# A state-space scan on eight cores: the C-product of one state moves from VectorE to GpSimd, the carry copy from GpSimd to ScalarE

## The reference

```python
def step(h, inp):                      # L = 2048 steps, d = 2048 channels, N = 16 states
    dt_t, B_t, C_t, x_t = inp
    A_bar = jnp.exp(jnp.minimum(dt_t[..., None] * A, 20.0))
    B_bar = dt_t[..., None] * B_t[:, None, :]
    h = A_bar * h + B_bar * x_t[..., None]
    y_t = jnp.einsum('bdn,bn->bd', h, C_t)
    return (h, y_t)
...
y = y + x_ssm * D[None, None, :]
y = y * jax.nn.silu(z)
out = jnp.einsum('ble,de->bld', y, W_out) * jax.nn.sigmoid(output_gate)
```

## Time and profile before

| | |
|---|---|
| time, 2 runs | 8252.49 and 8291.18 us, median 8271.84 us |
| the profiled execution's own time | 8309.93 us |
| its span, slowest core (5) | 8308.3 us; the other cores 8185.8 to 8300.3 us |
| DVE, POOL, PE, ACT busy | 45%, 37%, 26%, 14% of the span |
| granted TensorE clock, mean | 0.594 to 0.600 by core |
| scan stages, first to last block | 1828 to 7192 us |

### The profile page before, as it was taken

How to read it: one execution, slowest core, us unless ns; L and a number is a source line. 1 busy time by engine, 2 the same in 40 slices (tenths; PEclk the granted TensorE clock), 3 DMA queues, 4 the chain that set the end, 5 groups by cost and what they waited for, 6 DMA issues and landing times.

```text
span 8308.3 us, 37246 instructions; the slowest of 8 cores (8185.8 to 8308.3 us)
## 1 busy us (share of the span) xinstructions
PE 2185.6 (26%) x5698; PEld 533.1 (6%) x5698; DVE 3780.1 (45%) x3767; ACT 1148.8 (14%) x1666; POOL 3074.0 (37%) x3119
## 2 busy tenths in 40 slices
PE   0005657500000100346031007420400445034732
PEld 0001112100000000001010001000100000010101
DVE  0431111128888667586208676632468576201010
ACT  0001112102121111121101112110111121100000
POOL 0111111136666555463316454433355454300011
PEclk9998877655555555555565555555755555565556
DMA  8557665540000421020451200215321020433233
GB/s 112 161 148 155 147 143 130 125 81 8 9 9 10 58 51 32 14 51 7 72 81 40 62 23 13 48 28 83 81 53 32 14 50 12 72 84 78 41 62 70
DMA packets 851754, 529.48 MB, mean 64 GB/s; under 512 B 677762, under 2 KB 782210, under 8 KB 850882
## 3 DMA queue, kind: packets, MB, share of 16 engines
q0 software_dynamic: 122384, 262.35, 16.1%
q1 hardware_dynamic: 710706, 247.99, 13.8%
q10 hardware_dynamic: 18432, 16.79, 0.7%
HBM read 241.59 MB, written 144.97 MB: 47 GB/s over the span
## 4 chain that ended last, share of the span: by engine, by line
DVE 31%; DMA 31%; PE 11%; issue 9%; DVEq 7%; SPq 5%; POOL 3%; POOLq 3%; ACT 1%; ACTq 1%
DVE Hbz L215 20%; DVE ubz L215 7%; DVEq L213 7%; PE mid_ps L215 5%; PE big_ps L215 5%; DMA q2i_s<-qtt 4%; DMA q2sl<-q2i_s 4%; DMA wgi_s<-pt 3%; POOLq L213 2%; DMA wui_s<-pt 2%; DMA wdi_s<-pt 2%; SPq L832 2%; SPq L1017 2%; DMA pq<-wgi_s 1%; DMA pq<-wui_s 1%
## 5 line engine op out<-in xcount | busy, mean ns | idle before, releaser
L215 DVE TENSOR_TENSOR_SCAN Hbz<-abz,h_state,ubz 128x512 f32<-128x512 bf16 x1024 | 1900.6, 1856 | 79.7 <-issue 4.3
L215 POOL TENSOR_TENSOR yccz<-yccz,hcz 128x512 f32<-128x512 f32 x960 | 1401.1, 1459 | 145.1 <-issue 8.8
L215 POOL TENSOR_TENSOR hcz<-Hbz,Cb 128x512 bf16<-128x512 f32 x512 | 595.6, 1163 | 1908.5 <-DVE yccz L215 1063.5
L215 ACT ACTIVATE abz<-dtb,A_all 128x512 bf16<-128x512 bf16 x1024 | 740.7, 723 | 3509.6 <-DVE Hbz L215 1846.0
L215 PE MATMUL big_ps<-Wrg,xnF 128*128 128x512 bf16 x1024 | 604.2, 610 | 2177.7 <-DMA xnF<-iq_s 1766.2
L215 DVE TENSOR_TENSOR ubz<-wbs,Bb 128x512 bf16<-128x512 bf16 x1024 | 776.5, 758 | 133.9 <-ACT abz L215 66.1
L215 PE MATMUL mid_ps<-Wrg,xnF 128*128 128x512 bf16 x1024 | 604.5, 610 | 119.3 <-DVE sgb L215 47.4
L215 PE MATMUL mid_ps<-Wrg,q2F 128*128 128x512 bf16 x512 | 204.6, 400 | 1315.7 <-DMA q2F<-q_s 1315.7
L215 DVE TENSOR_SCALAR pt<-pwb,cols 128x1024 f32<-128x1024 f32 x96 | 72.3, 753 | 1005.2 <-DMA pwb<-w_u 349.6
L215 POOL COPY h_state<-Hbz 128x2 f32<-128x2 f32 x512 | 500.1, 977 | 0.0
L215 DVE SCALAR_TENSOR_TENSOR ob<-mid_ps,beta,ix 128x512 f32<-128x512 f32 x16 | 12.0, 751 | 981.8 <-PE big_ps L215 921.1
(11 more groups left out here) (107 smaller groups left out, 2304.8 us busy)
## 6 DMA issues: line engine op xcount, KB each, us to landing
pwb<-w_g POOLq DMA_DIRECT2D x64, 512.0 KB, 5.3
pwb<-w_u POOLq DMA_DIRECT2D x64, 512.0 KB, 5.1
pwb<-w_d POOLq DMA_DIRECT2D x64, 512.0 KB, 4.9
q2sl<-q2i_s POOLq DMA_DIRECT2D x128, 128.0 KB, 2.3
q_s<-q2sl POOLq DMA_DIRECT2D x128, 128.0 KB, 2.1
win_s<-w_in POOLq DMA_DIRECT2D x8, 1024.0 KB, 10.7
wdt_s<-w_dt POOLq DMA_DIRECT2D x4, 2048.0 KB, 19.2
xg<-x SPq DMA_DIRECT2D x16, 512.0 KB, 4.0
```

The lines of the kernel that those rows point to most:

```text
L215: r = _f(*a, **k)
```

## The change

Three things, all in the loop over pairs of states:
- The product `Hbz` * `Cb` of state n goes from DVE to POOL. POOL now waits for the scans' mark `tts_dv`, makes both products into `hcz`, and then the two adds; for the first pair of a block one add of both products into `yccz`.
- The copy of the two last columns into `h_state` goes from POOL to ACT. It is put into a list, `carry_pend`, and taken out in the next pair, between that pair's two Exp, behind a wait for the scans of the pair that it belongs to.
- DVE's wait for POOL ahead of its first `yccz` write goes with that write.

```diff
                         SCA.activation(sl(abz, p8), sl(dtb, s3), ACTF.Exp,
                                        scale=A_all[:, cn:cn + 1])
+                        if carry_pend:
+                            ccn, cap, cmk = carry_pend.pop(0)
+                            SCA.wait_ge(DV.sem, cmk)
+                            SCA.copy(h_state[:, ccn:ccn + 2], cap)
                         SCA.wait_ge(DV.sem, abz_free.get(p81, 0))
                         SCA.activation(sl(abz, p81), sl(dtb, s3), ACTF.Exp,
                                        scale=A_all[:, cn + 1:cn + 2])
@@
                         abz_free[p81] = tts_dv
-                        if n == 0:
-                            VEC.wait_ge(GP.sem, gp_n.get((ci - 1, N - 2), 0))
-                            VEC.tensor_tensor(sl(yccz, ci2), sl(Hbz, ph),
-                                              sl(Cb, n), ALU.mult)
-                        else:
-                            VEC.tensor_tensor(sl(hcz, ph), sl(Hbz, ph),
-                                              sl(Cb, n), ALU.mult)
-                        hc_dv = dv_mark()
-                        GPS.wait_ge(DV.sem, hc_dv)
+                        carry_pend.append(
+                            (cn, Hbz[:, ph * 512 + 511:ph * 512 + 1024:512],
+                             tts_dv))
+                        GPS.wait_ge(DV.sem, tts_dv)
+                        GPS.tensor_tensor(sl(hcz, ph), sl(Hbz, ph),
+                                          sl(Cb, n), ALU.mult)
                         GPS.tensor_tensor(sl(hcz, ph1), sl(Hbz, ph1),
                                           sl(Cb, n + 1), ALU.mult)
-                        if n > 0:
+                        if n == 0:
+                            GPS.tensor_tensor(sl(yccz, ci2), sl(hcz, ph),
+                                              sl(hcz, ph1), ALU.add)
+                        else:
                             GPS.tensor_tensor(sl(yccz, ci2), sl(yccz, ci2),
                                               sl(hcz, ph), ALU.add)
-                        GPS.tensor_tensor(sl(yccz, ci2), sl(yccz, ci2),
-                                          sl(hcz, ph1), ALU.add)
-                        GPS.tensor_copy(
-                            h_state[:, cn:cn + 2],
-                            Hbz[:, ph * 512 + 511:ph * 512 + 1024:512])
+                            GPS.tensor_tensor(sl(yccz, ci2), sl(yccz, ci2),
+                                              sl(hcz, ph1), ALU.add)
```

## The result

The changed kernel takes 8574.08 us (median of 11 runs, 8482 to 8618) against 8294.55 us before (10 runs): ratio 1.0304, interval 1.026 to 1.0348, **slower by 3.0%**. Every ratio in this document is taken from the fast runs alone (in a slower state, which three of these 11 runs show, some cores have a lower granted clock), so it need not be the quotient of the two medians; the fast runs here have a median of 8548 us. The forecast was 8544 us, 3.3% over the 8271.8 us then known. Timed once more beside two of the experiments the changed kernel gave 1.039 (1.0308 to 1.0472).

The account below looks back on a forecast made before the run. The common turns of DVE and POOL, 6.55 us a pair, were taken as the bound. 61 blocks at 4.31 us, 263, plus 9 at block heads gave 272 us over 8271.8: 8544 us, main range 8480 to 8620.

Parts of the forecast that it names:

- The turns: In the steady pair, DVE's and POOL's 128x512 operations alternate; their turns, 3.58 and 2.97 us, sum to the 6.55 us period.
- The product as a swap of 0.78 for 1.02 us: Per pair, DVE loses a 0.78 us product and POOL gains a 1.02 us turn: 6.55 to 6.79 us by turns alone.
- The wait for ACT: In every pair DVE waits for ACT's copy and second Exp after its second scan: 1.35 us, 1.15 to 1.87 at the bounds.
- POOL's first product free in the wait, `ubz` just ahead of the second: POOL's first product ends at 1.37 us; `ubz`, ready at 1.35, precedes the second product at 1.51; period 7.12 us.
- Head and tail: At 43 block heads the copy adds 0.20 us each, 9 us; each block's tail grows from 5.11 to 5.49 us.
- the late copy: Rival, chance 0.09: a wait over 1.51 us puts POOL's second product before the first `ubz`; period +1.17 us, 8802 us.
- The pauses: Behind block 12 of chunks 1 to 3, DVE waits for u-pieces anyway, so only 61 of 64 blocks pay 4.31 us.
- the sign that I had named as a failure: The forecast fails if the pauses between blocks shrink by more than those behind block 12.
- turns only: Rival, chance 0.10: POOL's turns use the whole wait in each pair; period 6.79 us, 2.0 us per block, 8394 us.
- Faster: Rival, chance 0.05: DVE's chain alone bounds, unheld by POOL; 0.78 us back in each of 7 pairs per block, 7961 us.
- Table loads: Rival, chance 0.04: the copy makes ACT reload its tables around each Exp, 1311 us more, 9583 us.

Follow-up runs that it names:

- the kernel with three copies: The changed kernel with ACT's copy done three times in a row in the same place: 8812.09 us, ratio 1.0707 to the kernel before.
- the kernel with the copy behind the mark: The changed kernel with ACT's copy behind the second Exp and its mark instead of between the two Exp: 8349.66 us, ratio 1.0123 to the kernel before.

## Why the prediction was right, step by step

- **The turns.** Right, and shown: taking POOL's adds away gave 0.919 where the sum of turns said near 0.92.
- **The product as a swap of 0.78 for 1.02 us.** Right in sign, too small in size where nothing else covers it. I had the pair at 6.79 us by turns alone; with the wait for ACT removed it is 6.93, 0.38 over before and not 0.24. The step took each turn at its length in the kernel before, where POOL had 1.02 us of rest per pair. With four POOL operations POOL never rests, and as I read it the 0.14 to 0.16 us between its instructions come onto the path. In the changed kernel this did not matter: POOL rests 1.29 us a pair there.
- **The wait for ACT.** 1.35 us forecast, 1.29 measured. The copy was taken at 0.20 and is 0.19; ACT starts it 0.09 us behind the scans' end, where I had 0.13.
- **POOL's first product free in the wait, `ubz` just ahead of the second.** Right, by a margin of 0.21 us: period 7.12 us, as worked out. With the wait at 1.64 us, in the kernel with three copies, it is 7.68.
- **Head and tail.** Tail right: 5.49 us from the scans' end to the D-fold, 5.11. Head too large: I added 0.20 us at 43 block heads. In the row pair below the second Exp's end moves by less, as copy and first Exp overlap; first Exp to `ubz` is 1.82 us, 1.74. A matter of 5 us in all.

```profile
2093.32 0.72 ACT L215 ACTIVATE abz<-dtb,A_all 128x512 bf16<-128x512 bf16 x1 [13.77 <-DMA dtb<-dt_s]
2093.95 0.18 ACT L215 COPY h_state<-Hbz 128x2 f32<-128x2 f32 x1
2094.20 1.52 ACT L215 ACTIVATE abz<-dtb,A_all 128x512 bf16<-128x512 bf16 x2
2095.14 0.92 DVE L215 TENSOR_TENSOR ubz<-wbs,Bb 128x512 bf16<-128x512 bf16 x2 [1.41 <-ACT abz L215]
```

- **A term that was missing.** Taken from the end of one pair's second scan to that of the next, the six steady periods of 64 blocks are 384: 334 of them are 7.0 to 7.2 us and 47 are over 7.3 (before, 14 are over 7.3, half of them in the first and last blocks of chunks). 21 of the 384 are near 7.68 us. One of these, seen from ACT:

```profile
2133.86 0.19 ACT L215 COPY h_state<-Hbz 128x2 f32<-128x2 f32 x1 [5.34 <-DVE Hbz L215]
2133.99 2.45 POOL L215 TENSOR_TENSOR hcz<-Hbz,Cb 128x512 bf16<-128x512 f32 x2 [1.29 <-DVE Hbz L215]
2134.40 1.52 ACT L215 ACTIVATE abz<-dtb,A_all 128x512 bf16<-128x512 bf16 x2 [0.35 <-issue]
2135.35 2.66 DVE L215 TENSOR_TENSOR ubz<-wbs,Bb 128x512 bf16<-128x512 bf16 x2 [1.57 <-ACT abz L215]
```

ACT stood still for 0.35 us, where 0.07 is usual, for nothing that the profile names; `ubz` came after POOL's second product, and the period was 7.68: the late copy, in single pairs. In all 21 the first `ubz` starts 0.25 to 0.73 us later than usual; in 6 the time is lost between ACT's copy and Exp, in 4 ahead of the copy, and in 11 between the Exp's end and `ubz`. The kernel before has six such pauses of 0.35 us ahead of a second Exp too, but there ACT was four pairs ahead. The 64 blocks took 3974 us from `wbs` to the end of `yinsl`, 3665 before: +309 us, where the sum had 64 x 4.31 = 276 and 9 for the heads. The difference of 24 us is a term that the sum put at nothing: 16 us are irregular periods among the 384 beyond those of before, the 21 among them, and 8 lie in the second pairs, which grew by 0.64 us on average and not by 0.51. The errors of the other terms are smaller and cancel.

- **The pauses.** The sum counted 61 blocks, since DVE waits behind block 12 anyway, and so took 13 us off. All pauses between blocks together, from the end of `yinsl` to the next `wbs`, are 1698 us before, but 1578 after and 1669 in a second profiled execution of the changed kernel. Those behind block 12 of chunks 1 to 3 went from 49.0, 52.8 and 49.8 us to 37.9, 36.4 and 37.7, and in the second execution to 43.8, 46.2 and 45.4. So 16 us in the second execution, near the 13 of the sum, and 40 in the first, where other pauses shrank as well; there the sign that I had named as a failure, pauses that shrink by more, did show. The `wu` loads in these pauses (issues, us to landing, slowest core) differ too. In the kernel before:

```profile
Wrg<-wu_s SPq DMA_TRANSPOSE x32, 7.9
```

in the changed kernel:

```profile
Wrg<-wu_s SPq DMA_TRANSPOSE x32, 6.8
```

and in the second profiled execution of the changed kernel:

```profile
Wrg<-wu_s SPq DMA_TRANSPOSE x32, 8.2
```

The scan stage, from the first `yinsl` to the last, is 5302.0 us before (1889.4 to 7191.4) and 5485.6 or 5577.3 after, +184 or +275. The blocks are alike in the two profiles after (992.8, 992.1 and 994.3 us for the first three chunks, against 992.7, 992.0 and 994.2); the pauses differ, with loads of 6.8 us in one and 8.2 in the other. One profile of each would by itself have said 2.2% (8487.5 to 8308.3), and the runs say 3.0%. What sets the speed of these loads in an execution stays open.

- **Where luck helped.** The blocks cost 309 us more and not the 285 of the sum, and the pauses gave back 30 to 121 us and not 13. The two misses go against each other, so a forecast of 3.3% between the two timings of 3.0 and 3.9% confirms the mechanism less closely than it looks. What confirms it are the steady period, the wait and the tail, each within 0.06 us.

Of the rivals, "turns only" (8394 us) fell with the wait of 1.29 us that POOL covers only in part; it is what the kernel with the copy behind the mark comes near to. "Late copy" did not set the period but shows in single pairs. "Faster" fell with the scans at 1834 ns. "Table loads" fell: 28 loads after, as in the earlier trace rows.

```profile
L215 ACT ACT_TABLE_LOAD x28 | 35.9, 1283 | 337.4 <-PE big_ps L215 200.1 <-DMA tiny<-gate 74.7 <-DMA dtb<-dt_s 61.5
```

## What to carry to other kernels

An instruction moved to an engine that is 14% busy is not free: look at what stands behind it in that queue, and whether it makes an engine that ran ahead wait for the one that it feeds. In the kernel before, the copy alone cost nothing one place further back (0.997) and 2.9% in its place. Where VectorE and GpSimd hold each other up as in this loop, count their time as one: moving the product from one to the other only swapped a short turn for a longer one, and what helped was fewer instructions, or an engine outside the pair.

## What the runs showed of the hardware that I had not expected

- Engines that take turns hide a part of each other's time: a scan takes 1.32 us alone but only 1.08 us after POOL's operation ends, a POOL add 1.15 alone and 0.94 in turn. So a pair in which DVE and POOL alternate is shorter than the sum of the lone durations.
- The irregular periods fall into the same pairs in both profiled executions of the changed kernel, on two different cores: the 47 over 7.3 us are the same 47, and the 21 near 7.68 the same 21. That points to the program and not to chance; the cause was not looked for.
- A bf16 product whose first input is read twice (128x1024 from 128x512) keeps the rate of the plain one: 0.68 us for 1024 elements a partition, 0.43 for 512.
